# Adjacency rows of a graph network: type-changing loads of GpSimd's queue, row sums later, more tiles moved by ScalarE

## What is computed

```python
# layer 0: mean over the neighbours
mask = (adj > 0).astype(x.dtype)
agg  = mask @ h / jnp.maximum(jnp.sum(mask, 1, keepdims=True), 1.0)
out  = relu(concat([h @ W_self + b_self, agg @ W_nb + b_nb]) @ W_comb + b_comb)
# layer 1: a gated network, 5 steps
Af, AfT = A.astype(f32), A.astype(f32).T
for _ in range(5):
    a_in, a_out = Af @ (state @ in_W.T + in_b), AfT @ (state @ out_W.T + out_b)
    # gates r, z and the candidate from concat([a_in, a_out, state]); state = (1-z)*state + z*h_hat
out = tanh(state @ o1_W.T + o1_b) @ o2_W.T + o2_b
```

## Time and profile before

| | before |
|---|---|
| median of 3 runs | 1223.17 us |
| the profiled execution, its own time | 1223.31 us |
| its span | 1221.5 us |
| TensorE busy | 1213.3 us (99%) |
| TensorE's weight loads | 604.9 us (50%) |
| VectorE busy | 745.9 us (61%) |
| ScalarE busy | 285.7 us (23%) |
| GpSimd busy | 17.5 us (1%) |
| DMA | 181.66 MB, mean 149 GB/s |
| GpSimd's queue (software) | 4.73 MB, 1.2% of 16 engines |
| SP's queue (hardware) | 175.91 MB, 39.7% of 16 engines |

### The profile page before, as it was taken

One profiled execution on the slowest core, in us unless ns is written; L12 is line 12 of the kernel. 1 busy time (PEld: TensorE's weight loads), 2 busy tenths in 40 slices (PEclk: granted clock), 3 DMA queues, 4 the chain that ended last, 5 costly groups with the idle time before them and its releaser, 6 DMA issues.

```text
span 1221.5 us, 12811 instructions
## 1 busy us (share of the span) xinstructions
PE 1213.3 (99%) x4836; PEld 604.9 (50%) x4836; DVE 745.9 (61%) x1241; ACT 285.7 (23%) x570; POOL 17.5 (1%) x18
## 2 busy tenths in 40 slices
PE   9999999999999999999999999999999999999999
PEld 6888644444444444444444444444444444444445
DVE  6668606778984573397267349636725864662674
ACT  4567200022331111033012113301202230220122
POOL 0400000000000000000000000000000000000000
PEclk9999999999999999999999999999999999999999
DMA  8555655850019405700830760191084039016202
GB/s 278 175 173 193 265 215 222 294 215 1 1 39 367 179 1 208 274 1 34 331 116 1 259 223 0 67 351 65 5 308 170 0 137 336 9 61 215 91 0 69
DMA packets 44969, 181.66 MB, mean 149 GB/s; under 512 B 3681, under 2 KB 13682, under 8 KB 29810
## 3 DMA queue, kind: packets, MB, share of 16 engines
q1 hardware_dynamic: 43440, 175.91, 39.7%
q0 software_dynamic: 1040, 4.73, 1.2%
q10 hardware_dynamic: 434, 0.27, 0.1%
HBM read 145.76 MB, written 35.14 MB: 148 GB/s over the span
## 4 chain that ended last, share of the span: by engine, by line
PE 86%; DVE 3%; issue 0%; ACT 0%; DVEq 0%
PE low_banks L404 42%; PE bank L404 42%; PE bank L619 1%; PE low_banks L619 0%; DVE LF L1337 0%; DVE GR L1484 0%; DVE first_GZ L1484 0%; DVE first_GH L1457 0%; DVE first_GZ L1487 0%; DVE GR L1487 0%; DVE ST L1460 0%; DVE u_buf L1521 0%; DVE GR L1441 0%; PE bank L549 0%; ACT GR L1049 0%
## 5 line engine op out<-in xcount | busy, mean ns | idle before, releaser
L404 PE MATMUL low_banks<-slot,LF 128*128 128x512 f16 x896 | 196.0, 379 | 0.0
L404 PE MATMUL bank<-slot,LF 128*128 128x512 f16 x896 | 194.7, 379 | 0.0
L404 PEld LDWEIGHTS bank<-slot,LF 128*128 128x128 f16 x896 | 87.7, 98 | 107.0 <-issue 2.3
L404 PEld LDWEIGHTS low_banks<-slot,LF 128*128 128x128 f16 x896 | 87.6, 98 | 103.1 <-DVE LF L1337 0.9
L404 PE MATMUL low_banks<-X,W 128*128 128x512 f32 x192 | 90.3, 592 | 0.0
L404 PE MATMUL bank<-X,W 128*128 128x512 f32 x192 | 90.2, 592 | 0.0
L404 PE MATMUL low_banks<-hi_lo,DR 128*128 128x256 f16 (+1 forms) x512 | 68.9, 275 | 3.2 <-DVE DR L1172 2.1
L404 PE MATMUL low_banks<-XT,W 128*128 128x512 f32 x144 | 67.7, 592 | 0.0
L404 PE MATMUL bank<-XT,W 128*128 128x512 f32 x144 | 67.7, 592 | 0.0
L404 PEld LDWEIGHTS low_banks<-X,W 128*128 128x128 f32 x192 | 36.2, 190 | 44.9 <-issue 44.3
L404 PEld LDWEIGHTS bank<-X,W 128*128 128x128 f32 x192 | 36.2, 190 | 43.1 <-issue 42.6
(11 more groups left out here) (306 smaller groups left out, 1720.1 us busy)
## 6 DMA issues: line engine op xcount, KB each, us to landing
slot<-quad_d SPq DMA_DIRECT2D x112, 1024.0 KB, 5.0
WG<-in_adj SPq DMA_DIRECT2D x32, 512.0 KB, 4.2
quad_d<-AT SPq DMA_DIRECT2D x12, 1024.0 KB, 5.0
quad_d<-A SPq DMA_DIRECT2D x12, 1024.0 KB, 9.6
quad_d<-spare SPq DMA_DIRECT2D x4, 1024.0 KB, 4.0
SN<-in_x SPq DMA_DIRECT2D x4, 512.0 KB, 8.3
x_d<-SN POOLq DMA_DIRECT2D x4, 512.0 KB, 4.2
x1o<-x_d SPq DMA_DIRECT2D x1, 2048.0 KB, 8.1
```

What stands on the lines that cost most here:

```text
L404: return pe.matmul(o, l, r, start=start, stop=stop, skip_group_check=again)
```

## The change

The ring, its semaphores and its loads go. GpSimd's queue loads adj straight into A, with a change of type from int32 to fp16 on the way, in 16 transfers, each of 512 rows by 512 columns (load_rows). Blocks 0 and 1 start when the third quarter of x is there; blocks 2 and 3, whose place held weights, after the store of the fused weights, once setup_done and bias_made are reached, and ahead of the stores of x1. TensorE's turning waits for the transfer alone. ScalarE's conversions go; in their place stand 64 row sums (row_sum), which copy A into an unused place for the sake of the accumulator: 24 in blocks 1 to 3 at odd tiles, 40 behind the last stage. ScalarE moves all turned tiles with i % 4 != 1: 48 instead of 38. The reduction of the sums moves on VectorE to just ahead of its first evacuation, TensorE's turning of them into spread(2), and ScalarE's copy behind its second evacuation.

```diff
-RING = 3
-ACT_MOVES = [i for i in range(NT * NB) if i % 2 == 0 or (i >= NT and i % NT in (3, 11))]
+ACT_MOVES = [i for i in range(NT * NB) if i % 4 != 1]
-        ring = wflat[:, 16:16 + RING * 1024].bitcast(INT32).rearrange("p (s r w) -> p s r w", s=RING, r=2)
+        unused = wflat[:, 16:16 + 2 * BN].bitcast(FP16).rearrange("p (s n) -> p s n", s=4)
...
 # sync
-            for k in range(2 * 4 * NB):
-                b, c, h = k // 8, k // 2 % 4, k % 2
-                if k >= RING:
-                    sp.wait_ge(conv, 2 * (k - RING + 1))
-                sp.dma_start(ring[:, k % RING, :, :], adj_v[b, c, h]).then_inc(ld_ring[k % RING], 16)
-            sp.wait_ge(conv, 4 * NT)
...
 # gpsimd
+            adj_v = adj.rearrange("(b q p) (c w) -> b c p q w", b=NB, q=BT, p=P, c=4)
+            def load_rows(b):
+                for c in range(4):
+                    pool.dma_start(A[:, c, BT * b:BT * b + BT, :], adj_v[b, c]).then_inc(ld_adj[4 * b + c], 16)
+            pool.wait_ge(ld_x[2], 16)
+            load_rows(0)
+            load_rows(1)
             pool.wait_ge(ld_c, 48)
...
             pool.dma_start(fused_d, fusedS).then_inc(st_fused, 16)
+            pool.wait_ge(setup_done, 1)
+            pool.wait_ge(bias_made, 1)
+            load_rows(2)
+            load_rows(3)
             for b in range(NB):
                 pool.wait_ge(x1_ready, BT * (b + 1))
...
 # tensor, turn_adj
-                pe.wait_ge(conv, 4 * (4 * b + m // 4 + 1))
+                pe.wait_ge(ld_adj[4 * b + m // BT], 16)
...
-            pe.wait_ge(degs_ready, 2)
-            pe.wait_ge(own_kept, 2 * NB)
-            pe.transpose(bank[7][0:2 * NT, 0:P], degs..., ident).then_inc(deg_turned, 1)
             spread(0, 6, NT - BT)
...
+            pe.wait_ge(own_kept, 2 * NB)
+            spread(1, 0, NT).then_inc(agg_done, 1)
+            pe.wait_ge(pq_act, 2)
+            pe.wait_ge(pq_dve, 2)
+            spread(2, 0, BT)
+            pe.wait_ge(pq_act, 4)
+            pe.wait_ge(pq_dve, 4)
+            pe.wait_ge(degs_ready, 2)
+            pe.transpose(bank[7][0:2 * NT, 0:P], degs..., ident).then_inc(deg_turned, 1)
+            spread(2, BT, NT).then_inc(agg_done, 1)
             pe.wait_ge(deg_kept, 1)
+            spread(3, 0, NT).then_inc(agg_done, 1)
...
 # scalar
+            def row_sum(e):
+                k, t = e // BT, BT * (e // NT) + e % BT
+                act.wait_ge(ld_adj[k], 16)
+                if e >= 4:
+                    act.wait_ge(row_sums, e - 3)
+                copy(unused[:, e % 4, :], A[:, k % 4, t, :], accum_out=degA[:, t, k % 4:k % 4 + 1]).then_inc(row_sums, 1)
...
             for i in range(NT * NB):
-                k = 2 * (i // 4 + 1) + i % 4 // 2
-                if k < 8 * NB:
-                    convert(k, i % 2)
                 if i in ACT_MOVES and i:
                     move_adj(i)
...
+                if i % 2 == 1 and i >= NT:
+                    row_sum((i - NT) // 2)
                 if i >= NT and i % NT in STAGE_AT:
                     block_end(i // NT - 1)[STAGE_AT.index(i % NT)]()
...
+            for e in range((NT * NB - NT) // 2, NT * NB):
+                row_sum(e)
...
 # vector, ahead of out_pq(0)
+            dve.wait_ge(row_sums, NT * NB)
+            v.tensor_reduce(degs[:, 0, :], degA[:, :, :], mybir.AxisListType.X, ALU.add).then_inc(degs_ready, 1)
+            v.tensor_reduce(degs[:, 1, :], degT[:, :, :], mybir.AxisListType.X, ALU.add).then_inc(degs_ready, 1)
```

More of the change, by code:

```diff
@@ L175, in graph_net @@
         ld_wo = [sem(f"ld_wo{j}") for j in range(2)]
-        ld_ring = [sem(f"ld_ring{i}") for i in range(RING)]
+        ld_adj = [sem(f"ld_adj{i}") for i in range(4 * NB)]
         st_fused, st_x1, st_out = sem("st_fused"), sem("st_x1"), sem("st_out")
@@ L193, in graph_net @@
         hT_ready, hT_act, hT_dve = sem("hT_ready"), sem("hT_act"), sem("hT_dve")
-        conv = sem("conv")
+        row_sums = sem("row_sums")
         tr_ready = sem("tr_ready")
@@ L301, in _ @@
             sp.dma_start(ioR[:, 1, 1, :], w_out[P:2 * P, :]).then_inc(ld_wo[1], 16)
-            adj_v = adj.rearrange("(b h r p) (c w) -> b c h p r w", b=NB, h=2, r=2, p=P, c=4)
-            for k in range(2 * 4 * NB):
-                b, c, h = k // 8, k // 2 % 4, k % 2
-                if k >= RING:
-                    sp.wait_ge(conv, 2 * (k - RING + 1))
-                sp.dma_start(ring[:, k % RING, :, :], adj_v[b, c, h]).then_inc(ld_ring[k % RING], 16)
-            sp.wait_ge(conv, 4 * NT)
             sp.wait_ge(at_act, len(ACT_MOVES))
@@ L798, in _ @@
             turn_h2(NB - 1, 1)
-            pe.wait_ge(degs_ready, 2)
-            pe.wait_ge(own_kept, 2 * NB)
-            pe.transpose(bank[7][0:2 * NT, 0:P], degs[:, :, :].rearrange("p w t -> p (w t)"),
-                         ident).then_inc(deg_turned, 1)
             spread(0, 6, NT - BT)
@@ L808, in _ @@
             pe.wait_ge(s_dve, NB)
-            pe.wait_ge(deg_kept, 1)
[L810 to L814, removed]
+            pe.wait_ge(own_kept, 2 * NB)
[6 more added lines that the diff above has]
+            pe.wait_ge(degs_ready, 2)
+            pe.transpose(bank[7][0:2 * NT, 0:P], degs[:, :, :].rearrange("p w t -> p (w t)"),
+                         ident).then_inc(deg_turned, 1)
+            spread(2, BT, NT).then_inc(agg_done, 1)
+            pe.wait_ge(deg_kept, 1)
+            spread(3, 0, NT).then_inc(agg_done, 1)
             for n in range(FIRST, 2 * (STEPS - 1)):
@@ L925, in _ @@
             move_h(0)
[L926 to L929, removed]
             fused(2)
@@ L971, in _ @@
                 stage()
-            act.wait_ge(deg_turned, 1)
-            copy(deg16[:, :], bank[7][0:2 * NT, 0:P]).then_inc(deg_kept, 1)
+            for e in range((NT * NB - NT) // 2, NT * NB):
+                row_sum(e)
             def out_pq(b):
@@ L1057, in _ @@
                 out_pq(b)
+                if b == 1:
+                    act.wait_ge(deg_turned, 1)
+                    copy(deg16[:, :], bank[7][0:2 * NT, 0:P]).then_inc(deg_kept, 1)
             for n in range(FIRST, 2 * (STEPS - 1)):
@@ L1295, in _ @@
             residual(NB - 1, 0, BT)
-            dve.wait_ge(conv, 4 * NT)
             dve.wait_ge(at_act, len(ACT_MOVES))
@@ L1300, in _ @@
             variance(range(BT * (NB - 1), NT), BT * (NB - 1))
-            v.tensor_reduce(degs[:, 0, :], degA[:, :, :], mybir.AxisListType.X, ALU.add).then_inc(degs_ready, 1)
-            v.tensor_reduce(degs[:, 1, :], degT[:, :, :], mybir.AxisListType.X, ALU.add).then_inc(degs_ready, 1)
             newton(0, BT, NB + 3, 0.5 / SCALE)
```

## The result

The changed kernel takes 1232.6 us (median of 4 runs, 1231.24 to 1232.77 us), the kernel before 1223.2 us. The ratio on record is 1.0083, 95% interval 1.0071 to 1.0095; the two medians themselves are 9.4 us apart (1.0077), and 6.3 us were forecast. The profiled execution took 1232.5 us, its span is 1230.7 us, 9.2 us longer than that of before.

A forecast was written before the change was run, and what follows sets the result against it. TensorE, busy 1213.3 of 1221.5 us, was taken as the bound. Stall 4.8, clock 1.7 and block 0 0.7, less 1.2 in blocks 2 and 3, add 6.0 us to 1223.2 us, rounded up to 1229.5 us; range 1220.5 to 1250 us.

The forecast's parts named there:

- likeliest case: Store of x1 held behind the loads at the full rate: 1229.5 us, own range 1227 to 1233 us, chance 0.48.
- block 0: Adjacency stage, first block: masks of tiles moved by ScalarE come a turn later, +0.7 us, bounds 0 and 1.5 us.
- the stall: TensorE's second turning of h2 in block 0 waits for the held x1 store, until 88.9 us: 4.8 us lost.
- the clock: TensorE's rest of some 5 us lowers its clock behind it: 1.7 us, bounds 0 and 1.7 us.
- Rival B: GpSimd's queue: the x1 store isn't held, 1222.2 us (1221 to 1223.5 us), chance 0.17.
- Rival C: Store not held and most of TensorE's waits go, clearly faster: 1217 to 1220.7 us, chance 0.11.
- Rival A: Loads of adj: the type change slows the transfers, 1235 to 1255 us, chance 0.24.
- Part 1: Adjacency stage: 64 conversions leave ScalarE, 39.6 us of records; alone this gives TensorE nothing.
- Part 2: Ten more moves for ScalarE: masks come earlier in blocks 1 to 3, 0.6 us gained a block; block 0 loses 0.7 us.
- part 4: Start of the loads: chunk 0 lands at 20.9 us, in time, cost nothing; an issue takes 0.6 to 2.4 us.
- Part 3: Row sums behind ScalarE's last stage and later degrees: 16 us of cover, broadcast lands near 220 us, cost nothing.
- Part 5: GpSimd's queue: the x1 store waits behind 8.91 MB of loads at 377 GB/s, lands at 87.2 us, loss 4.8 us.

The follow-up runs named there:

- e7: Changed kernel with x1 stores of blocks 0 to 2 on SP's queue and all moves divided as in the kernel before: 1223.48 us, ratio 1.0019.
- e8: e1 with block 0's old division of moves, 48 row sums beside tiles of blocks 1 to 3, degrees at their old places: 1221.35 us, ratio 0.9997.
- e1: Changed kernel with the x1 stores of blocks 0 to 2 issued by SP's queue instead of GpSimd's: 1223.70 us, ratio 1.0014.
- e5: e1 without the two broadcasts of the degrees, the vectors they fill zeroed by VectorE: 1222.31 us, ratio 1.0003.
- e9: e8 with the four loads of block 1 issued behind the fused store: 1220.73 us, ratio 0.9993.
- e4: Changed kernel with plain fp16 loads of adj, half the bytes read and as many written: 1223.29 us, ratio 1.0010.
- e3: Changed kernel with 50 zero products on TensorE ahead of its wait for block 0's turned state: 1230.41 us, ratio 1.0070.

## Why the prediction was right, and where its terms were off

The mechanism, its place and its sign were as forecast, and the time lies in the range, near the top of the likeliest case's own (1227 to 1233 us). The forecast was 3.1 us short, which is four terms that were all sized too small: block 0 was 0.9 us dearer, the stall 0.9 us, the clock 0.75 us, the degrees 0.6 us. Rival B would have had the store land before 82 us; it landed at 89.0 us. Rival C needed B. Rival A would have shown less than 300 GB/s read; there were 410 GB/s.

**Part 1** held: e7, without conversions and with the old division of the moves, has blocks as long as before.

**Part 2, blocks 1 to 3**, held to the tenth: 0.62 and 0.61 us in blocks 2 and 3. **In block 0** the price was 1.6 us, not 0.7 us. Two steps failed. The start: the first mean came at 27.70 instead of 27.39 us, which I had at nothing in part 4; VectorE's L1108 and L1113 (the lines L1111 and L1116 of e8) took longer beside the issues and TensorE waited 1.62 instead of 1.14 us. Tile 7: I had 0.1 us; measured was 0.7 us, of it 0.54 us as a listed wait, and one tile later than I looked. VectorE's timeline of the changed kernel:

```profile
44.65 0.29 DVE L1170 TENSOR_SCALAR DR<-AT 128x512 f16<-128x512 f16 x1
44.86 1.12 DVE L1232 SCALAR_TENSOR_TENSOR A<-A,col 128x256 f32<-128x256 f32 x1
46.01 0.41 DVE L1237 TENSOR_TENSOR A<-A 1x256 f32<-1x256 f32 x1
46.35 0.85 DVE L1170 TENSOR_SCALAR DR<-AT 128x512 f16<-128x512 f16 x1
```

The row arithmetic of the bias (L1232) now starts at 44.86 us instead of 44.16 us and takes 1.12 us instead of 0.47 us, the row behind it 0.41 instead of 1.00 us, and the mask 0.85 instead of 0.27 us: 2.3 us for the three instead of 1.7 us. GpSimd's arithmetic runs beside them in both kernels (42.55 to 47.06 us now, 42.09 to 46.70 us before), so that is not new; in both, VectorE's long masks (0.45 to 1.40 us instead of 0.28 us) start within GpSimd's arithmetic, and which operation is long moves with the start. No run takes GpSimd's arithmetic away, so that it is the cause is read from the coincidence. Tile 11 was sized right (0.44 us, of it 0.28 us as a listed wait, against 0.4), tile 3 too (0.2 us). The step that failed: the working of part 2 moves operations in time and keeps the durations of their old rows, but these do not stay. Start, tile 3, tile 7 and tile 11 together are the 1.6 us.

**Part 3** was wrong in "nothing again, even at double price". Cover was reckoned for the reader of the broadcasts, and there it held. Nobody looked at the queue beside them: their 157 us were a free place, 204 to 213 us lies beside the stores of quarters, which VectorE waits for. Price 0.6 us here, 1.2 to 1.5 us once the stall is gone (e1 against e5), which is when a reader would meet it.

**Part 4** held for the landing (TensorE never waited for a first chunk) and for the issue, 0.74 to 0.78 us against bounds of 0.6 and 2.4 us.

**Part 5** held in its large sum, and there luck had a part, since two errors of opposite sign cancelled: from the first issue at 62.70 us to the landing at 89.0 us it took 26.3 us, 26.4 us were forecast, though the rate in a full queue was 410 and not 377 GB/s; 8.91 MB at 410 GB/s are 21.7 us, so 4.6 us and not 2.8 us were fixed (the first data moved 1.4 us after the issue, and until 65.3 us no more than 133 GB/s was written). That reading sets the rate, as this part took it, is not shown: no run separates it from the change of type. Around the sum were 0.9 us more in all: 0.3 us between the last bias column and the first issue, and 0.7 us behind the landing, where a row sum with its accumulator read stands in ScalarE's queue between the state and the turned state (90.10 to 90.71 us). Part 3 had put it there; I had counted the row sums as a block of 40 and forgotten the one in the gap. The sum also took the early fall of the clock as part of both times; it lies ahead of the stall and is swallowed by it, as the gain of block 1 is, so against executions without the fall the stall is 7.2 us. **The clock** cost 2.4 us, not 1.7 us: it came back 5.1 us after work did.

By the rule of the Trainium skill (DMA: Bandwidth & Descriptors, Anatomy of one DMA) the queue would have moved 436 GB/s; the trace shows 410 GB/s read once it runs and 26.3 us for the whole, so what weighed against it was less the rate than the start. The other page of the Trainium skill, SBUF — State Buffer, Who interferes with whom, has VectorE starve the writing of descriptors; it also says that whichever of the two comes first holds the shared ports while the other stands. No run here shows the issues delayed, eight took 5.94 us beside VectorE's masks; what e8 and e9 show is the other direction, VectorE slowed beside them.

## What to carry to other kernels

Before moving traffic onto a queue, write down what stands behind it there and who waits for its landing; small stores that someone waits for belong ahead of prefetches or on another queue. Look at a moved transfer from both sides: whether it is in time for its reader, and whom it now runs beside. When a change bundles parts, try the cheapest one alone: here one line of it, on the old kernel, gained 1.5 us (0.12%), which none of the mended versions of the whole surpassed.

## What the runs showed of the hardware

- Loads that change int32 to fp16 on the way read 410 GB/s with 2 KB runs, 2061 runs in 10 us on 16 engines, 78 ns for each. Plain int32 loads of the kernel before, on SP's queue, were no faster (377 GB/s). Plain fp16 loads of the same bytes written go in a quarter of the packets, at 325 GB/s (e4).
- GpSimd issues a transfer of 512 runs in 0.74 to 0.78 us, one of 128 runs in 0.59 us: four times the runs, not four times the time. Beside such issues some of VectorE's scalings take 1.47 to 1.67 us instead of 1.38 us for four.
- A rest of 5.7 us took the clock to 1.2 GHz some 4 us into it, and it stayed there for 5.1 us of full work; with 50 products in that place and 1.9 us of rest left it stayed at 2.4 GHz (e3). Behind the one-column products the clock falls in some executions and not in others.
- The broadcasts of the degrees lengthen the landing of stores beside them: 10.9 us (e1) instead of 6.9 us (e5, without them).
